# A two-layer-type graph network on one core: five slots a layer fetched row by row from two queues, in place of two from one

## The reference

```python
msg = jax.nn.relu(x[src] + edge_attr)
agg = jax.ops.segment_sum(msg, dst, num_segments=N_NODES)
h = (x + agg) @ W1l + b1l
h = (h - mean(h)) * rsqrt(var(h) + BN_EPS) * gl + bl
h = relu(relu(relu(h) @ W2l + b2l))
```

```python
agg = jax.ops.segment_sum(x[src], dst, num_segments=x.shape[0])
h = relu(((1.0 + eps) * x + agg) @ wA.T + bA) @ wB.T + bB
```

## Time and profile before

| What | us |
|---|---|
| median of 3 runs | 2755.7 (2754.37 to 2758.44) |
| the profiled execution | 2753.93 |
| its span | 2752.1 |

### The profile page before, as it was taken

One profiled execution on the slowest core, in us unless ns is written; L12 is line 12 of the kernel. 1 busy time (PEld: TensorE's weight loads), 2 busy tenths in 40 slices (PEclk: granted clock), 3 DMA queues, 4 the chain that ended last, 5 costly groups with the idle time before them and its releaser, 6 DMA issues.

```text
span 2752.1 us, 35065 instructions
## 1 busy us (share of the span) xinstructions
PE 1908.3 (69%) x9399; PEld 1278.4 (46%) x9399; DVE 1701.1 (62%) x2880; ACT 735.4 (27%) x1002; POOL 1941.4 (71%) x2048
## 2 busy tenths in 40 slices
PE   2476656566656672666566666656578999989999
PEld 2354444344444442435444444434444566546555
DVE  7797677777777764777777777777774221342212
ACT  4132222222222251333333333333361000210001
POOL 6777777777777727777777777777707777377773
PEclk8687777787888786878878888888878999999999
DMA  6343433343434333444444444444426566465653
GB/s 199 97 144 107 129 107 122 113 128 114 135 114 136 120 112 98 132 138 127 149 128 149 135 156 141 156 149 149 146 92 203 190 219 198 135 208 186 211 193 101
DMA packets 228544, 396.82 MB, mean 144 GB/s; under 512 B 43080, under 2 KB 133020, under 8 KB 228388
## 3 DMA queue, kind: packets, MB, share of 16 engines
q0 software_dynamic: 65024, 133.30, 18.1%
q1 hardware_dynamic: 111684, 162.15, 17.2%
q10 hardware_dynamic: 51680, 99.63, 10.4%
HBM read 333.10 MB, written 61.81 MB: 143 GB/s over the span
## 4 chain that ended last, share of the span: by engine, by line
POOL 52%; PE 22%; issue 18%; DVE 4%; DMA 3%; ACT 1%; DVEq 1%; POOLq 0%; SPq 0%; ACTq 0%
POOL xg L675 50%; PE psA L1537 14%; PE psG L1552 4%; POOL xg L695 2%; DMA xg<-node_table,src_all 2%; PE psG L1601 2%; PE psA L1609 1%; DVE xp_room L1131 0%; DVE hid L1077 0%; PE psG L1631 0%; DVE acc L1030 0%; DVE hid L1247 0%; PE psA L1618 0%; DVE xp_room L955 0%; DVEq L1052 0%
## 5 line engine op out<-in xcount | busy, mean ns | idle before, releaser
L675 POOL DMA_INDIRECT xg<-node_table,src_all x1520 | 1437.3, 946 | 506.9 <-issue 458.3
L1510 PE MATMUL psG<-hid,xp_room 128*128 128x160 f32 x3072 | 614.2, 376 | 421.6 <-DVE hid L1077 411.7
L1510 PEld LDWEIGHTS psG<-hid,xp_room 128*128 128x128 f32 x3072 | 595.3, 255 | 466.3 <-issue 455.8
L1494 PE MATMUL psA<-cell_room,xp_room 128*128 128x512 f16 (+1 forms) x2336 | 551.6, 388 | 299.2 <-ACT count_out L742 253.3
L1117 DVE TENSOR_SCALAR cell_room<-psG,cell_all 128x932 f16<-128x932 int16 x1088 | 684.6, 688 | 0.0
L695 POOL DMA_INDIRECT xg<-node_table,idx x480 | 468.1, 975 | 250.6 <-issue 248.7
L759 ACT COPY psG<-xp_room 128x512 f32<-128x512 f32 x384 | 226.5, 590 | 1257.7 <-DVE xp_room L1131 1226.5
L1494 PEld LDWEIGHTS psA<-cell_room,xp_room 128*128 128x128 f16 x2336 | 230.7, 103 | 582.7 <-ACT count_out L742 287.8
L1131 DVE TENSOR_TENSOR xp_room<-psG,xg 128x512 f32<-128x512 f32 x380 | 257.3, 677 | 385.8 <-DMA xg<-node_table,src_all 372.2
L1030 DVE TENSOR_TENSOR acc<-acc,row_slot 128x38 f32 x192 | 38.7, 202 | 385.3 <-ACT row_slot L838 360.7
L1077 DVE SCALAR_TENSOR_TENSOR hid<-loc_all,round_off,psG 128x2560 f32<-128x2560 f32 x96 | 274.7, 2862 | 0.1
(11 more groups left out here) (156 smaller groups left out, 804.5 us busy)
## 6 DMA issues: line engine op xcount, KB each, us to landing
xp_room<-in_edge_attr_dram ACTq DMA_DIRECT2D x95, 768.0 KB
cell_room<-count_store SPq DMA_DIRECT2D x16, 2850.0 KB
count_store<-count_out SPq DMA_DIRECT2D x96, 465.5 KB
hid<-count_store SPq DMA_DIRECT2D x16, 2736.0 KB
xg<-node_table,src_all POOLq DMA_INDIRECT x1520
xp_room<-in_edge_attr_dram ACTq DMA_DIRECT2D x95, 256.0 KB
row_slot<-node_table SPq DMA_DIRECT2D x1024, 0.5 KB
hid<-node_table SPq DMA_DIRECT2D x1024, 0.5 KB
```

Source lines behind the costliest of these rows:

```text
L675: nc.gpsimd.indirect_dma_start(xg[:, n % XG, u, j, :], None, x if n < RAW_TURNS else table, bass.IndirectOffsetOnAxis(ap=src_all[:, s, j:j ...
L1494: last = nc.tensor.matmul(psA[:, bank, 0:w], src_hot[:, hots(n) % 2, at, :], cells[:, c % CELL_RING, c0:c0 + w], start=first, stop=end)
L1510: last = nc.tensor.matmul(psG[:, q, h * WIN:(h + 1) * WIN], ea[:, t, u, j, :], rows[:, u, j, :], start=(u == slots[0] and j == 0), stop=(u ...
```

## The change

Three constants change. Five slots of each of the layers 0 and 1 are fetched by rows, those of turns 13, 22, 30, 39 and 48, in place of turns 26 and 48. SyncE fetches for 11 partitions a turn, 44 rows, in place of 6 and 24, and ScalarE for one partition at each of the four slots, 16 rows a turn. Five slots have 640 partitions, which is 43 turns at 15 a turn, as two slots were 43 turns at 6. The list of addresses that SyncE loads at the start has five parts in place of two.

```diff
-ROW_TURNS = (26, TURNS - 1)
+ROW_TURNS = (13, 22, 30, 39, TURNS - 1)
 ROW_START = 3
-BY_SYNC = 6
-ACT_GROUPS = ((0, 0), (0, 0))
+BY_SYNC = 11
+ACT_GROUPS = ((1, 1), (1, 1))
 BY_ACT = sum(map(sum, ACT_GROUPS))
 ROW_STEP = BY_SYNC + BY_ACT
```

## The result

The changed kernel takes 2759.24 us (median of 12 runs, 2755.69 to 2763.95), the kernel before 2754.26 us beside it. The ratio is 1.0017, 95% interval [1.001, 1.0025]: slower by 0.17%, where 2726 us was forecast. One of the 12 runs of the kernel before took 6318.41 us; the ratio leaves it out, and what held it up is not known. The profiled execution took 2756.8 us, of which 2755.0 are the span. So the question is where 30 us of removed gathers went.

A forecast was written before the change was run, and what follows sets the result against it. POOL's steady stream of gathers was taken to bound layers 0 and 1. 2753.9 - 30.0 for the gathers, nothing for all other parts, gave 2723.9 us, 2726 on the median's scale; range 2718 to 2747 us.

The forecast's parts named there:

- Gathers: POOL in layers 0 and 1: 24 gathers fewer at 1.249 us each, 30.0 us saved, all on the path.
- SyncE: SyncE's queue, 44 rows a turn: 808 us in layer 0, 843 in layer 1, against POOL's 840; cost nothing.
- 18.6 us to spare: End of layer 1: SyncE's fetching ends at 1938.6 us, the last turn's row slot is summed after 1957.2.
- Rival 2: SyncE's queue merely level: count stores late, ScalarE waits to evict; some 14 us come back, 2740 us; chance 0.15.
- ScalarE: ScalarE's queue: 16 rows and 2.2 loads, 7.1 us a turn, hide in its waits of 12.3 us; cost nothing.
- Rival 1: SyncE and ScalarE share one descriptor generator, rows come late: 241 us added, 2967 us; chance 0.07.
- Rival 3: ScalarE's queue: fetches at the upper bound exceed its waits by 0.9 us; 21 us come back, 2747 us; chance 0.07.
- Rival 4: DMA engines: all 60 rows of a turn on one engine fill it, 267 us added, 2993 us; chance 0.03.

## Why the prediction was wrong

**Gathers: right.** 24 fewer, at the price given, with POOL waiting for nothing new of weight (46.8 us for the table, 3.0 for VectorE). Where the queues have room the whole 30 us appear: 30.4 us with 36 and 24 rows, 27.2 with 40 and 20.

**SyncE: the step that failed.** It is the sentence "I put SyncE at nothing, with the least cover of all parts". Two things in it were wrong.

First, the deadline. The 18.6 us to spare were measured to the last row slot, the latest thing that waits for SyncE's rows. But the rows are not "needed only at the end": each of the five slots is summed in its own turn. VectorE waited for the slot of turn 13 in layer 0 and for that of turn 30 in layer 1:

```profile
DVE xp_room L1131 <- DMA row_slot<-node_table: 6.7, 1, 6.7
DVE xp_room L1131 <- DMA hid<-node_table: 5.2, 1, 5.2
```

The count stores stand in the same queue and are wanted much sooner; the paragraph named them as what waits behind the rows and then gave them no margin of their own. The profile after shows which deadline bound: those two waits are 11.9 us in all, while ScalarE waited 142.0 us for stores.

Second, the size of a turn. By the prediction's prices a turn with 44 rows and two stores is 44 x 0.317 + 150 / 43 x 0.46 + 44 x 0.059 + 2 x 0.38 + 0.92 = 19.8 us. It took 21.2. The five turns above show where the 1.4 us are: from the end of the stores to the first fetch 3.03 us in the mean, where 0.92 and a load of 1.40 were put (0.71 more), the stretch of 44 fetches 17.29 us, where 16.75 were put (0.54 more), and 0.14 around the stores. Over layer 1 the fetching lasted from 1100.07 to 1984.90 us, 885 us with 14 of waiting for evictions in them, where 843 were put. And the average over a layer hid the point: layer 1's 843 us against POOL's 840 looked level, but the layer has two kinds of turns. Those with two stores, 23 of the 43, are few at first, roughly alternate with turns of one store from turn 19 of the layer on, and stand ten in a row at its end. From SyncE's timeline of layer 1:

```profile
1100.07 16.56 SPq L573 DMA_DIRECT2D hid<-node_table  x44
...
1428.91 0.85 SPq L587 DMA_DIRECT2D count_store<-count_out  x2
1432.84 17.54 SPq L573 DMA_DIRECT2D row_slot<-node_table  x44
1450.43 0.38 SPq L587 DMA_DIRECT2D count_store<-count_out  x1
...
1469.49 0.85 SPq L587 DMA_DIRECT2D count_store<-count_out  x2
...
1968.89 16.01 SPq L573 DMA_DIRECT2D hid<-node_table  x40
```

From the stores at 1428.91 us to those at 1925.21 us lie 24 turns, 17 with two stores at 21.2 us in the mean and 7 with one at 19.5. SyncE's queue took 496.3 us for them without a pause; POOL's stream, with three row turns among them, allows 24 x 20.0 - 3 x 5.0 = 465 us. The queue falls behind by 31 us there, which is what layer 1 lost.

**Rival 2: the right mechanism, too small.** It had late stores, ScalarE waiting to evict, and PE behind it, at a chance of 0.15. Its price of 14 us came from dearer loads less the same 18.6 us of spare; what the runs show is a loss of 33 us (2759.24 against 2726). Without the spare that the stores did not have, its own sum, 33 us over POOL's time, would have come to the measured size. That agreement would have been luck: it got there by dearer loads all along, while the loads within a turn kept their price (0.93 us for 8 values and 1.39 for 16 in the median) and half of the excess lies in the gap after two stores.

**ScalarE: right.** Its fetches and SyncE's, by source:

```profile
L780 ACTq DMA_DIRECT2D row_slot<-node_table x672: 234/235/1015, 124.7 to 1763.8; - x168
...
L573 SPq DMA_DIRECT2D row_slot<-node_table x1888: 224/228/822, 85.1 to 1804.0; - x189
```

Four rows took 1.2 to 1.5 us in the timeline, 0.30 to 0.38 each, where 0.317 was taken, and the kernel before with 32 rows a turn on ScalarE ran in the same time as without.

**Rival 1: fell as a mechanism.** SyncE's fetches take 228 ns in the median as in the earlier trace rows, with ScalarE fetching beside them, and ScalarE's 235, as they did where ScalarE fetched alone; the attribute loads of ScalarE took 385 ns at least, 412 in the median (385 before) and 439 at most. Some issues are longer, up to 1197 ns on SyncE and 1015 on ScalarE. In the mean SyncE's fetches went from 233 to 235 ns, some 9 us over both layers, where the rival put 157 in each; ScalarE's took 281 ns, against 254 alone, and its waits had room for that. The rule of the Trainium skill (Perfetto Trace Analysis, DMA Instruction — HWDGE) that the wait for a shared generator's lock stands inside the reported time would have shown as longer issues; the medians show none, and the means no more than this. **Rival 3** has its own run with seven slots; at the change's 16 rows it is far off. **Rival 4** fell: 72 rows a turn with six slots run at 2716 us, so no DMA engine fills up at 60.

## What to carry to other kernels

A queue's issue time is a resource like an engine's: before a queue is given more, add up everything that it issues in its fullest turn, address loads and gaps included, and set it against the turn, not the average against the layer. Slack is measured to the earliest thing that waits for anything in that queue, here a store of another data path, not to the last use of what was added. Where a queue is nearly full, four rows of 60 moved to a queue with room decided over nearly all of the 30 us, and moving the urgent stores out did as well.

## What was not expected

The first fetch after a store comes late by an uneven gap: after two stores 2.7 to 3.7 us in the five turns above, after single stores in layer 0 of the change 0.6 to 2.9 us. An address load is in each gap, and its size explains most of the spread. With 4 values the gap was 0.64 us in the median after one store, with 16 values 2.17 after one store and 3.03 after two, against 1.39 where no store went before. It is the load itself that is longer: 16 values took 1.26 us elsewhere in the turn, 2.04 after one store and 2.90 after two (medians of 131, 27 and 13 loads). In the fetching turns of layer 1 of the kernel before, two stores of a turn went out 5.5 to 9.4 us apart, since SyncE waited for the second eviction, and the gap behind the second was 2.21 us in the median of 17. So no row of before could show what two stores issued back to back cost the load behind them. Why they make it longer was not tried.

TensorE's granted clock fell as well: 0.77 in the mean between 1700 and 1980 us, a mixture of stretches at its two levels, 1.2 and 2.4 GHz, against 0.84 before and 0.84 again with 40 rows. The engine was busy for 162 of these 280 us and waited longer for ScalarE's evictions, so the clock looks like a consequence of the waits; no run sets it apart.

The loss is steep: between 40 and 48 rows a turn on SyncE the time rises by 141 us. By the turns above a row costs (22.4 - 19.1) / 8 = 0.4 us with its share of loads, and it is paid in every turn in which this queue is the slowest.
